# Chunked cross-attention on one core: scores and probabilities times values placed together, and every engine's list reordered

## The chip, the cores and the metric

The kernel runs on one core of a Trainium2 chip. The metric is device time in microseconds of one execution; three runs of the kernel before gave 1942.81, 1947.82 and 1955.28 us, median 1947.82 us. The profile is one further execution, whose span from first to last instruction is 1939.0 us.

## The reference

Batches of 32, channels 256, tokens 2048. Queries, keys and values all come from the context tensor; attention is within chunks of 64 tokens, with 8 heads of 32 channels.

```python
qh, kh, vh = proj(ctx, Wq, bq), proj(ctx, Wk, bk), proj(ctx, Wv, bv)   # in chunks of 64
scores = einsum('bnqhd,bnkhd->bnhqk', qh, kh) / sqrt(32)
scores = scores + where(mask > 0, 0, -1e9)
attn   = softmax(scores)
out    = einsum('bnhqk,bnkhd->bnqhd', attn, vh) @ W_out.T + b_out
out    = out.transpose(0, 2, 1) * mask + x
mu, var = mean and variance over the 2048 tokens
return (out - mu) * rsqrt(var + 1e-5)
```

## The kernel before, in words

The work is cut into 128 blocks of 512 tokens, four to a batch. Each engine runs its own straight list of instructions, written out by a Python loop `periods(step)`; one step is called a round here. In round p the engines work on different blocks at once: the projections on block p+2, the softmax on p+1, the turned probabilities on p, the product with values on p-1, the output projection on p-2. Nothing but semaphores joins the engines, and each engine goes through its list in the written order. So the order of the calls in the five `step` functions, together with the waits, is the whole schedule.

The stages of one block, in the order in which they depend on each other:

- ScalarE (ACT) rounds the context to `ctx_hi` (`split_ctx`, L458); GpSimd (POOL) forms the rest `ctx_lo` (`low_ctx`, L565). Products are made of three terms, hi by hi, hi by lo, lo by hi.
- TensorE (PE) projects keys and queries (L313, 24 matmuls) and values (L347, 24) into two banks `proj_bank`, of which each half f is emptied by ACT (`keys` L500, `queries` L491, `values` L508).
- POOL turns the mask into rows of 0 or a large negative number (`masked_keys`, L587), and ACT lays these into the four banks `score_bank` in two halves (`lay_negatives`, L470). TensorE adds the scores on top (`scores`, L386, 64 small matmuls).
- VectorE (DVE) takes the row maximum and subtracts it (`less_maximum`, L646, L650); ACT takes the exponential in two halves (`exponentials`, L478); DVE sums each half and forms reciprocals (`sum_up` L657, `reciprocals` L665); POOL multiplies in two halves (`divide`, L557).
- DVE transposes the probabilities in 32x32 squares (`turn`, L673), and eight transfers from the queue of SyncE (SP) put the squares in place (`move_probs`, L256). TensorE multiplies by the values (`probs_times_v`, L419), half of which were carried to the other partitions by two transfers (`move_values`, L241).
- ACT and DVE split the result (`high_attention` L485, `low_attention` L680), TensorE projects it (`project_out`, L370), DVE adds bias and mask (`output`, L691), POOL adds x (`add_residual`, L575), DVE gathers statistics (L700), and after four blocks ACT and POOL normalise (L520, L598) and SP stores.

Two waits matter for what follows. `lay_negatives(n, 0)` waits for `neg_done`, that is for `masked_keys(n)`, and for `less_done` of the block before. `divide(n, 0)` waits for `recip_done` of block n, which needs both halves of the exponentials of block n.

Of the kernel before, what the change touches and what calls it, by code (L numbers as in the profile page):

```python
# [14 lines left out]
HALVES = C // P  # L15
# [35 lines left out]
def attention_kernel(nc, x, ctx_in, mask, w_in_t, b_in, w_out_t, b_out, out):  # L51
    stack = ExitStack()
    with stack:
# [127 lines left out]
        def periods(step):  # L181
            for p in range(-3, ALL + 4):
                step(p)

        @block.sync
        def _(sp):
# [58 lines left out]
            def move_probs(n):  # L245
# [26 lines left out]
            def step(p):  # L272

                move_values(p + 1)
                if p >= -2:
                    load_ctx(p + 6)
                if there(p + 2):
                    sp.wait_ge(q_proj, 2 * (p + 2) + 1)
                if p >= -1:
                    load_mask(p + 3)  # L280
                if there(p + 2):
                    sp.wait_ge(q_proj, 2 * (p + 2) + 2)
                if p >= 3:
                    load_x(p - 1)
                move_probs(p)

                if p == ALL + 2:
                    for n in range(p - 7, ALL):
                        store(n)
                elif p < ALL + 2:  # L290
                    store(p - 7)
# [7 lines left out]
        def _(pe):  # L299
# [17 lines left out]

            def project_k(n, f):
                if not there(n):
                    return  # L320
                if f == 0:
                    pe.wait_ge(ctx_hi_done, 2 * (n + 1))
                    pe.wait_ge(ctx_lo_done, 2 * (n + 1) - 1)
                    if n == 0:
                        pe.wait_ge(ctx_lo_first, 1)
                wait(pe, v_f_done, 2 * (n - 1) + f + 1 if n else 0)
# [8 lines left out]
            def project_v(n, f):  # L335
                if not there(n):
                    return
                if there(n - 4):
                    pe.wait_ge(y_done, 2 * (n - 4) + f + 1)
                else:  # L340
                    pe.wait_ge(q_f_done, 2 * n + f + 1)
# [10 lines left out]
            def project_out(m, f):  # L352
# [6 lines left out]
                if there(m + 4):  # L359
                    pe.wait_ge(q_f_done, 2 * (m + 4) + f + 1)  # L360
                elif there(m + 3):
# [12 lines left out]
            def scores(n):  # L374
# [3 lines left out]
                pe.wait_ge(k_f_done, 2 * (n + 1))  # L378

                pe.wait_ge(seeded, 2 * (n + 1))  # L380
# [22 lines left out]
            def probs_times_v(n):  # L403
# [8 lines left out]
                pe.wait_ge(moved[n % MOVES], 128 * (n // MOVES + 1))  # L412
                for c in range(CPB):
# [36 lines left out]
        def _(act):  # L450
# [72 lines left out]
            def step(p):  # L523
                keys(p + 2, 0)
                split_ctx(p + 3, 0)
                keys(p + 2, 1)
                split_ctx(p + 3, 1)
                queries(p + 2, 0)
                queries(p + 2, 1)
                exponentials(p + 1, 0)  # L530
                exponentials(p + 1, 1)
                lay_negatives(p + 2, 0)
                lay_negatives(p + 2, 1)
                high_attention(p - 1)
                values(p + 2, 0)
                if p == ALL + 2:
                    for n in range(p - 7, ALL):
                        normalise(n)
                elif p < ALL + 2:
                    normalise(p - 7)  # L540
                values(p + 2, 1)
# [4 lines left out]
        def _(pool):  # L546
# [54 lines left out]
            def step(p):  # L601
                if p < 0:
                    masked_keys(p + 2)
                low_ctx(p + 3, 0)
# [3 lines left out]
                if p < ALL + 2:  # L608
                    normalise(p - 7)
# [161 lines left out]
```

## Time and profile before

| what | value |
|---|---|
| runs | 1942.81, 1947.82, 1955.28 us |
| span of the profiled execution | 1939.0 us |
| TensorE busy | 98% |
| VectorE busy | 88% |
| GpSimd busy | 78% |
| ScalarE busy | 69% |
| chain that ended last, share of TensorE | 96% |

The page prints only the span of the profiled execution; its own time is that span and what lies around it, and the median of the runs is 8.8 us above the span. A busy share counts only instructions that compute. The chain that ended last is followed backward from the last instruction, at each step to whatever released it.

### The profile page before, as it was taken

Reading aid. Unit: us, or ns where it says so; the run is one execution under the profiler, and the core shown is the slowest. Engines: PE = TensorE matmul, PEld = TensorE weight load, DVE = VectorE, ACT = ScalarE, POOL = GpSimd, SP = SyncE. Lnnn points to the kernel's source line nnn. Section 1 sums busy time; section 2 is a strip of 40 time slices with the busy share of each in tenths; the row PEclk is TensorE's granted clock in tenths of the full one; section 3 lists DMA queues with packets and bytes.
Section 4 is the critical chain, followed back from the end, with each engine's and each line's share of the span. In section 5 each row is a group of like instructions: output and inputs, shape, how many; then the busy total and the mean of one; then the engine's idle time right before and its main releaser. Section 6 shows DMA issues by size and latency. Waiting matters only on the chain.

```text
span 1939.0 us, 90624 instructions
## 1 busy us (share of the span) xinstructions
PE 1891.7 (98%) x40488; PEld 1608.1 (83%) x40488; DVE 1703.2 (88%) x1577; ACT 1330.1 (69%) x1792; POOL 1504.6 (78%) x1059
## 2 busy tenths in 40 slices
PE   7999999999999999999999999999999999999994
PEld 6888888888888888888888888888888888888882
DVE  4898889899999978998988999888899889989986
ACT  5667667767767766776777677677667767767762
POOL 4677778878888778878777887787778778778874
PEclk9999999999999999999999999999999999999997
DMA  5667778777777767777777777777777777777766
GB/s 171 159 181 215 218 206 224 215 218 223 212 220 222 213 196 217 222 215 215 221 219 212 221 222 214 222 210 215 212 221 219 215 217 216 222 209 222 208 176 195
DMA packets 242882, 409.60 MB, mean 211 GB/s; under 512 B 28992, under 2 KB 94784, under 8 KB 242496
## 3 DMA queue, kind: packets, MB, share of 16 engines
q1 hardware_dynamic: 242496, 403.82, 74.2%
q8 instruction: 320, 5.24, 1.2%
q14 instruction: 66, 0.54, 0.1%
HBM read 168.82 MB, written 67.11 MB: 122 GB/s over the span
## 4 chain that ended last, share of the span: by engine, by line
PE 96%; DVE 1%; issue 1%; ACT 1%; DMA 0%; POOL 0%; SPq 0%; DVEq 0%
PE proj_bank L313 38%; PE proj_bank L370 19%; PE proj_bank L347 19%; PE score_bank L386 11%; PE o_bank L419 9%; DMA b_cols<-b_in 0%; ACT prob L478 0%; ACT score_bank L470 0%; DVE squares L673 0%; SPq L256 0%; POOL prob L557 0%; DVE stats L700 0%; POOL y L575 0%; DMA prob_t<-squares 0%; DVE sums L657 0%
## 5 line engine op out<-in xcount | busy, mean ns | idle before, releaser
L557 POOL TENSOR_TENSOR prob<-prob,recip 128x1024 f32<-128x1024 f32 x256 | 482.0, 1904 | 46.5 <-DVE recip L665 46.5
L575 POOL TENSOR_TENSOR y<-y,x_raw 128x512 f32<-128x512 f32 x256 | 331.5, 1295 | 181.1 <-DVE y L691 181.1
L565 POOL TENSOR_TENSOR ctx_lo<-ctx_raw,ctx_hi 128x512 fp32r<-128x512 f32 x255 | 330.2, 1295 | 171.9 <-ACT ctx_hi L458 159.7
L500 ACT ACTIVATE k_f<-proj_bank,b_cols 128x512 f32<-128x512 f32 x256 | 176.4, 689 | 365.2 <-PE proj_bank L313 365.2
L646 DVE TENSOR_REDUCE row_max<-score_bank 128x32 f32<-128x2048 f32 x128 | 293.4, 2292 | 138.7 <-PE score_bank L386 138.7
L313 PE MATMUL proj_bank<-ctx_hi,w_hi 128*128 128x512 f32 x1024 | 337.1, 410 | 3.0 <-DVE ctx_lo L630 3.0
L313 PE MATMUL proj_bank<-ctx_hi,w_lo 128*128 128x512 f32 x1024 | 322.1, 396 | 0.7 <-issue 0.7
L313 PE MATMUL proj_bank<-ctx_lo,w_hi 128*128 128x512 f32 x1024 | 322.1, 396 | 0.0
L657 DVE TENSOR_REDUCE sums<-prob 128x16 f32<-128x1024 f32 x256 | 309.3, 1209 | 5.0 <-ACT prob L478 5.0
L650 DVE TENSOR_TENSOR prob<-score_bank,row_max 128x2048 f32<-128x2048 f32 x128 | 293.3, 2292 | 4.4
L673 DVE STREAM_TRANSPOSE squares<-prob 128x2048 f32<-128x2048 f32 x128 | 294.6, 2301 | 2.6 <-POOL prob L557 2.6
L478 ACT ACTIVATE prob<-prob 128x1024 f32<-128x1024 f32 x256 | 255.2, 1047 | 5.6 <-DVE prob L650 5.6
L491 ACT ACTIVATE q_f<-proj_bank,b_cols 128x512 f32<-128x512 f32 x256 | 176.4, 689 | 115.1 <-PE proj_bank L313 115.1
L470 ACT ACTIVATE score_bank<-neg_rows 128x1024 f32<-128x1024 f32 x256 | 251.3, 1016 | 0.0
L587 POOL TENSOR_SCALAR neg_rows<-mask_all 128x512 f32<-128x512 f32 x128 | 247.0, 1929 | 2.5 <-DMA mask_all<-mask 2.5
L691 DVE SCALAR_TENSOR_TENSOR y<-proj_bank,b_final,mask_all 128x512 f32<-128x512 f32 x256 | 190.3, 744 | 49.8 <-PE proj_bank L370 49.8
L313 PEld LDWEIGHTS proj_bank<-ctx_hi,w_lo 128*128 128x128 f32 x1024 | 194.0, 189 | 46.9 <-issue 1.0
L313 PEld LDWEIGHTS proj_bank<-ctx_lo,w_hi 128*128 128x128 f32 x1024 | 193.5, 189 | 45.2
L313 PEld LDWEIGHTS proj_bank<-ctx_hi,w_hi 128*128 128x128 f32 x1024 | 183.9, 189 | 46.5 <-issue 3.7
L386 PE MATMUL score_bank<-k_f,q_f 32*64 32x64 f32 x16384 | 214.7, 233 | 3.0 <-ACT score_bank L470 2.8
L386 PEld LDWEIGHTS score_bank<-k_f,q_f 32*64 32x64 f32 x16384 | 196.7, 130 | 21.3 <-issue 3.8
L419 PEld LDWEIGHTS o_bank<-prob_t,v_f 64*32 64x32 f32 x8192 | 169.8, 105 | 51.2 <-issue 51.2
(45 smaller groups left out, 3487.1 us busy)
## 6 DMA issues: line engine op xcount, KB each, us to landing
prob_t<-squares SPq DMA_DIRECT2D x1024, 128.0 KB
ctx_raw<-ctx SPq DMA_DIRECT2D x128, 512.0 KB, 4.8
x_raw<-x SPq DMA_DIRECT2D x128, 512.0 KB, 4.8
out<-y SPq DMA_DIRECT2D x128, 512.0 KB, 4.3
mask_all<-mask SPq DMA_DIRECT2D x128, 256.0 KB, 4.2
v_x<-v_f SPq DMA_DIRECT2D x256, 128.0 KB, 3.4
y<-w_in_t SPq DMA_DIRECT2D x1, 768.0 KB, 5.6
y<-w_out_t SPq DMA_DIRECT2D x1, 256.0 KB, 6.7
```

The lines of the kernel that those rows point to most:

```text
L313: last = pe.matmul(proj_bank[:, f, :], w[:, h, col + f * P:col + (f + 1) * P], c[:, n % 2, h, :], start=(a == 0 and h == 0), stop=(a == 2 ...
L347: last = pe.matmul(proj_bank[:, f, t * C:(t + 1) * C], c[:, n % 2, h, tok:tok + P], w[:, h, 2 * C:3 * C], start=(a == 0 and h == 0), stop= ...
L370: last = pe.matmul(proj_bank[:, f, :], w[:, h, f * P:(f + 1) * P], o[:, m % 2, :, h, :], start=(a == 0 and h == 0), stop=(a == 2 and h == 1))
L386: last = pe.matmul(score_bank[f * CHUNK:(f + 1) * CHUNK, r, tokens], q_f[head, n % 2, f, tokens], k_f[head, n % 2, f, tokens], start=False ...
L419: last = pe.matmul(o_bank[r * DH:(r + 1) * DH, f, c * CHUNK:(c + 1) * CHUNK], values, prob_t[keys, :, r * CPB + c, :], start=True, stop=Tr ...
L557: pool.tensor_tensor(part, part, half(slots(recip[:, n % 2, :]), i), ALU.mult).then_inc(norm_done, 1)
L565: pool.tensor_tensor(ctx_lo[:, n % 2, :, tokens], ctx_raw[:, n % BLOCKS, :, tokens], ctx_hi[:, n % 2, :, tokens].bitcast(F32), ALU.subtrac ...
L575: pool.tensor_tensor(part, part, x_raw[:, m % 2, f, :], ALU.add).then_inc(added, 1)
L646: dve.tensor_reduce(row_max[:, :].rearrange("p (r c) -> p r c", c=CPB), scores_of, AX_X, ALU.max).then_inc(max_done, 1)
L650: dve.tensor_tensor(prob[:, n % 2, :, :, :], scores_of, slots(row_max[:, :]), ALU.subtract).then_inc(less_done, 1)
L657: dve.tensor_reduce(sums[:, i * SLOTS // 2:(i + 1) * SLOTS // 2], half(prob[:, n % 2, :, :, :], i).rearrange("p r c k -> p (r c) k"), AX_X ...
L673: dve.transpose(squares[:, :, :, :], prob[:, n % 2, :, :, :].rearrange("p r c (b j) -> p b (r c) j", j=SQ)).then_inc(turned, 1)
```

## The change

On TensorE the product with values of block p-1 comes directly behind the scores of block p+1, and all waits of the two are placed ahead of the scores. The output projection of block p-1 (before: p-2) comes at the end of the round, so that product and output projection of a block fall in the same round. The projection banks are therefore handed on in another sequence: K waits for the output of block n-4, V for the queries. `turn` is cut in two halves b, each with its own semaphore count, and `move_probs` sends four transfers behind each half. ACT, POOL, DVE and SP get new orders. The loop runs two rounds fewer.

```diff
@@ periods
-            for p in range(-3, ALL + 4):
+            for p in range(-3, ALL + 2):
@@ move_probs (SP)
-                sp.wait_ge(turned, n + 1)
                 wait(sp, pv_done, n)
-                for f in range(HALVES):
-                    for a in range(2):
-                        for b in range(2):
+                for b in range(2):
+                    sp.wait_ge(turned, 2 * n + b + 1)
+                    for f in range(HALVES):
+                        for a in range(2):
@@ step (SP)
-                move_values(p + 1)
-                if p >= -2:
-                    load_ctx(p + 6)
...
+                store(p - 7)
+                if there(p + 2):
+                    sp.wait_ge(k_proj, 2 * (p + 2) + 1)
                 if p >= -2:
                     load_ctx(p + 6)
+                move_probs(p)
+                if p >= 3:
+                    load_x(p - 1)
+                move_values(p + 2)
                 if p >= -1:
                     load_mask(p + 3)
@@ step (PE)
                 met(PIECE_WAITS)
+                context_ready(p + 2)
+                rows_ready(p + 1)
+                probs_ready(p - 1)
                 scores(p + 1)
+                probs_times_v(p - 1)
                 project_k(p + 2, 0)
                 project_k(p + 2, 1)
                 project_q(p + 2, 0)
                 project_q(p + 2, 1)
                 if p == -1:
                     output_bias()
-                project_out(p - 2, 0)
-                probs_times_v(p - 1)
-                project_out(p - 2, 1)
                 project_v(p + 2, 0)
                 project_v(p + 2, 1)
+                project_out(p - 1, 0)
+                project_out(p - 1, 1)
@@ step (ACT)
+                split_ctx(p + 3, 0)
+                split_ctx(p + 3, 1)
+                high_attention(p - 1)
                 keys(p + 2, 0)
-                split_ctx(p + 3, 0)
                 keys(p + 2, 1)
-                split_ctx(p + 3, 1)
+                lay_negatives(p + 2, 0)
                 queries(p + 2, 0)
+                exponentials(p + 1, 0)
                 queries(p + 2, 1)
-                exponentials(p + 1, 0)
                 exponentials(p + 1, 1)
-                lay_negatives(p + 2, 0)
+                values(p + 2, 0)
+                values(p + 2, 1)
                 lay_negatives(p + 2, 1)
-                high_attention(p - 1)
-                values(p + 2, 0)
...
+                    normalise(p - 6)
@@ step (POOL)
                 if p < 0:
                     masked_keys(p + 2)
+                add_residual(p - 2, 0)
+                add_residual(p - 2, 1)
                 low_ctx(p + 3, 0)
                 low_ctx(p + 3, 1)
                 if p >= 0:
                     masked_keys(p + 2)
...
-                add_residual(p - 2, 0)
-                add_residual(p - 2, 1)
                 divide(p + 1, 0)
                 divide(p + 1, 1)
@@ step (DVE)
-                turn(p)
-                statistics(p - 3)
...
+                turn(p, 0)
+                turn(p, 1)
+                low_attention(p - 1)
+                statistics(p - 2)
...
-                output(p - 2, 0)
                 sum_up(p + 1, 0)
-                output(p - 2, 1)
                 sum_up(p + 1, 1)
                 reciprocals(p + 1)
-                low_attention(p - 1)
+                output(p - 1, 0)
...
+                output(p - 1, 1)
```

The list of ACT before, one round in the middle of the program (names are output<-inputs; k_f, q_f, v_f are keys, queries, values of block p+2; `prob` is block p+1, `score_bank` p+2):

```order
L500 ACTIVATE k_f<-proj_bank,b_cols 128x512 [waits rows_done,k_proj]
L458 ACTIVATE ctx_hi<-ctx_raw 128x2x256 [waits v_proj,ctx_loaded2]
L500 ACTIVATE k_f<-proj_bank,b_cols 128x512 [waits rows_done,k_proj]
L458 ACTIVATE ctx_hi<-ctx_raw 128x2x256
L491 ACTIVATE q_f<-proj_bank,b_cols 128x512 [waits q_proj] x2
L478 ACTIVATE prob<-prob 128x1024 [waits less_done] x2
L470 ACTIVATE score_bank<-neg_rows 128x1024 [waits less_done,neg_done]
L470 ACTIVATE score_bank<-neg_rows 128x1024
```

The same list after the change (its lines are six higher: L476 is `lay_negatives`, L484 `exponentials`, L497 `queries`):

```order
L491 ACTIVATE o_hi<-o_bank 128x1024 [waits out_proj,pv_done]
L506 ACTIVATE k_f<-proj_bank,b_cols 128x512 [waits rows_done,k_proj] x2
L476 ACTIVATE score_bank<-neg_rows 128x1024 [waits less_done,neg_done]
L497 ACTIVATE q_f<-proj_bank,b_cols 128x512 [waits q_proj]
L484 ACTIVATE prob<-prob 128x1024 [waits less_done]
L497 ACTIVATE q_f<-proj_bank,b_cols 128x512 [waits q_proj]
L484 ACTIVATE prob<-prob 128x1024 [waits less_done]
L514 ACTIVATE v_f<-proj_bank 128x512 [waits pv_done,v_proj] x2
L476 ACTIVATE score_bank<-neg_rows 128x1024
```

The first half of the laying of block p+2, with its wait for `neg_done`, has moved from behind both exponentials of block p+1 to ahead of both; the second half stands behind the values.

The list of POOL before, in the same place (prob is `divide`, ctx_lo is `low_ctx`, neg_rows is `masked_keys`, the two y lines are `normalise` and `add_residual`):

```order
L557 TENSOR_TENSOR prob<-prob,recip 128x1024 [waits recip_done]
L557 TENSOR_TENSOR prob<-prob,recip 128x1024
L565 TENSOR_TENSOR ctx_lo<-ctx_raw,ctx_hi 128x2x256 [waits ctx_hi_done] x2
L587 TENSOR_SCALAR neg_rows<-mask_all 128x512 [waits seeded,mask_loaded1]
L598 TENSOR_SCALAR y<-y,rstd,shift 128x512 [waits shift_done]
L575 TENSOR_TENSOR y<-y,x_raw 128x512 [waits x_loaded1,y_done]
L575 TENSOR_TENSOR y<-y,x_raw 128x512 [waits y_done]
```

And after the change (lines six higher):

```order
L563 TENSOR_TENSOR prob<-prob,recip 128x1024 [waits recip_done]
L563 TENSOR_TENSOR prob<-prob,recip 128x1024
L581 TENSOR_TENSOR y<-y,x_raw 128x512 [waits x_loaded1,y_done]
L581 TENSOR_TENSOR y<-y,x_raw 128x512 [waits y_done]
L571 TENSOR_TENSOR ctx_lo<-ctx_raw,ctx_hi 128x2x256 [waits ctx_hi_done] x2
L593 TENSOR_SCALAR neg_rows<-mask_all 128x512 [waits seeded,mask_loaded1]
L604 TENSOR_SCALAR y<-y,rstd,shift 128x512
```

The two residual additions now stand between the divisions and `masked_keys`, whose place behind `low_ctx` is kept.

## Rows read from the trace of the kernel before

**Rows 1.** The chain that ended last, one round: start, us, what.

```profile
721.09 1.40 PE proj_bank L370 x6
722.49 1.41 PE o_bank L419 x91
723.90 1.58 PE proj_bank L370 x6
725.49 2.88 PE proj_bank L347 x24
728.36 1.57 PE score_bank L386 x91
729.93 5.77 PE proj_bank L313 x24
```

**Rows 2.** Timeline of ACT in a round: start us, us, instruction.

```profile
1014.09 0.69 ACT L491 ACTIVATE q_f<-proj_bank,b_cols 128x512 f32<-128x512 f32 x1 [0.71 <-PE proj_bank L313]
1014.68 1.99 ACT L478 ACTIVATE prob<-prob 128x1024 f32<-128x1024 f32 x2
1016.57 1.96 ACT L470 ACTIVATE score_bank<-neg_rows 128x1024 f32<-128x1024 f32 x2
```

**Rows 3.** Timeline of DVE in the same part.

```profile
1019.41 1.21 DVE L657 TENSOR_REDUCE sums<-prob 128x16 f32<-128x1024 f32 x1
1020.72 0.35 DVE L665 RECIPROCAL recip<-sums 128x32 f32<-128x32 f32 x1
...
1023.10 2.29 DVE L646 TENSOR_REDUCE row_max<-score_bank 128x32 f32<-128x2048 f32 x1 [0.71 <-PE score_bank L386]
...
1027.63 2.30 DVE L673 STREAM_TRANSPOSE squares<-prob 128x2048 f32<-128x2048 f32 x1
1029.86 1.25 DVE L700 BATCH_NORM_STATS2 stats<-y 128x6 f32<-128x512 f32 x2
```

**Rows 4.** Timeline of POOL in the same part, and two additions near the end.

```profile
1021.16 3.77 POOL L557 TENSOR_TENSOR prob<-prob,recip 128x1024 f32<-128x1024 f32 x2 [0.29 <-DVE recip L665]
1025.85 2.68 POOL L565 TENSOR_TENSOR ctx_lo<-ctx_raw,ctx_hi 128x512 fp32r<-128x512 f32 x2 [0.92 <-ACT ctx_hi L458]
1028.49 1.94 POOL L587 TENSOR_SCALAR neg_rows<-mask_all 128x512 f32<-128x512 f32 x1
...
1911.30 2.53 POOL L575 TENSOR_TENSOR y<-y,x_raw 128x512 f32<-128x512 f32 x2 [3.49 <-DVE y L691]
```

**Rows 5.** Timeline of SP: eight transfers of probabilities, twice.

```profile
1884.52 5.79 SPq L256 DMA_DIRECT2D prob_t<-squares  x8
...
1909.42 4.95 SPq L256 DMA_DIRECT2D prob_t<-squares  x8
```

**Rows 6.** TensorE in stretches: us, busy (instructions), granted clock, DMA share, GB/s.

```profile
44.50:46.30 1.80, 0.06 (x1) 1.00 0.87 200
47.00:53.00 6.00, 5.33 (x95) 0.50 0.63 156
262.00:264.00 2.00, 0.44 (x43) 1.00 0.40 135
704.00:706.00 2.00, 0.00 (x0) 0.91 0.54 196
706.00:712.00 6.00, 5.70 (x36) 0.50 0.47 108
```

**Rows 7.** Who waited for whom: us in total, times, longest.

```profile
PE o_bank L419 <- issue: 6.2, 4, 2.6
```

**Rows 8.** The chain near the end of the program.

```profile
1890.53 2.30 DVE row_max L646
...
1913.78 2.44 DMA prob_t<-squares
...
1918.03 2.87 PE proj_bank L370 x6
...
1921.67 1.13 DVE o_lo L680
```

**Rows 9.** Timeline of DVE, the first row maximum.

```profile
23.95 2.29 DVE L646 TENSOR_REDUCE row_max<-score_bank 128x32 f32<-128x2048 f32 x1 [10.69 <-PE score_bank L386]
```

More of the change, by code:

```diff
@@ L272, in step @@
             def step(p):
-                move_values(p + 1)
+                store(p - 7)
+                if there(p + 2):
+                    sp.wait_ge(k_proj, 2 * (p + 2) + 1)
                 if p >= -2:
                     load_ctx(p + 6)
-                if there(p + 2):
-                    sp.wait_ge(q_proj, 2 * (p + 2) + 1)
+                move_probs(p)
+                if p >= 3:
+                    load_x(p - 1)
+                move_values(p + 2)
                 if p >= -1:
                     load_mask(p + 3)
[L281 to L288, printed above, removed]
+                if p == ALL + 1:
+                    for n in range(p - 6, ALL):
                         store(n)
-                elif p < ALL + 2:
-                    store(p - 7)
             periods(step)
@@ L315, in project_qk, with context_ready @@
                 last.then_inc(proj, 1)
+            def context_ready(n):
+                if not there(n):
+                    return
+                pe.wait_ge(ctx_hi_done, 2 * (n + 1))
+                pe.wait_ge(ctx_lo_done, 2 * (n + 1) - 1)
+                if n == 0:
+                    pe.wait_ge(ctx_lo_first, 1)
             def project_k(n, f):
@@ L320, in project_k @@
                     return
[L321 to L326, printed above, removed]
+                if there(n - 4):
+                    pe.wait_ge(y_done, 2 * (n - 4) + f + 1)
+                else:
+                    wait(pe, v_f_done, 2 * (n - 1) + f + 1 if n else 0)
                 project_qk(n, f, k_proj, C)
@@ L337, in project_v @@
                     return
[L338 to L341, printed above, removed]
+                pe.wait_ge(q_f_done, 2 * n + f + 1)
                 for t in range(2):
@@ L358, in project_out @@
                     pe.wait_ge(o_hi_done, m + 1)
-                if there(m + 4):
-                    pe.wait_ge(q_f_done, 2 * (m + 4) + f + 1)
-                elif there(m + 3):
+                if there(m + 3):
                     pe.wait_ge(v_f_done, 2 * (m + 3) + f + 1)
@@ L372, in project_out, with rows_ready @@
                 last.then_inc(out_proj, 1)
-            def scores(n):
+            def rows_ready(n):
                 if not there(n):
@@ L380, in scores @@
                 pe.wait_ge(seeded, 2 * (n + 1))
+            def scores(n):
+                if not there(n):
+                    return
                 for c in range(CPB):
@@ L412, in probs_times_v @@
                 pe.wait_ge(moved[n % MOVES], 128 * (n // MOVES + 1))
+            def probs_times_v(n):
+                if not there(n):
+                    return
                 for c in range(CPB):
@@ L607, in step @@
                     masked_keys(p + 2)
-                if p < ALL + 2:
-                    normalise(p - 7)
-                if there(p - 3) and (p - 3) % BLOCKS == BLOCKS - 1:
-                    reciprocal_std((p - 3) // BLOCKS)
-                if p == ALL + 2:
-                    for n in range(p - 7, ALL):
+                if p < ALL + 1:
+                    normalise(p - 6)
+                if there(p - 2) and (p - 2) % BLOCKS == BLOCKS - 1:
+                    reciprocal_std((p - 2) // BLOCKS)
+                if p == ALL + 1:
+                    for n in range(p - 6, ALL):
                         normalise(n)
-                add_residual(p - 2, 0)
-                add_residual(p - 2, 1)
                 divide(p + 1, 0)
@@ L665, in reciprocals, with turn @@
                 dve.reciprocal(recip[:, n % 2, :], sums[:, :]).then_inc(recip_done, 1)
-            def turn(n):
+            def turn(n, b):
                 if not there(n):
                     return
-                dve.wait_ge(norm_done, 2 * (n + 1))
-                if there(n - 1):
-                    dve.wait_ge(moved[(n - 1) % MOVES], 128 * ((n - 1) // MOVES + 1))
-                dve.transpose(squares[:, :, :, :], prob[:, n % 2, :, :, :].rearrange(
-                    "p r c (b j) -> p b (r c) j", j=SQ)).then_inc(turned, 1)
+                if b == 0:
+                    dve.wait_ge(norm_done, 2 * (n + 1))
+                    if there(n - 1):
+                        dve.wait_ge(moved[(n - 1) % MOVES], 128 * ((n - 1) // MOVES + 1))
+                dve.transpose(squares[:, b, :, :], prob[:, n % 2, :, :, b * SQ:(b + 1) * SQ].rearrange(
+                    "p r c j -> p (r c) j")).then_inc(turned, 1)
             def low_attention(m):
```

18 lines of the change are left out of this document (8 added, 10 removed).

## The prediction

> **What bounds the kernel now.** I read the page's table of busy times first, then the chain of waits, then the timelines of one round. TensorE is busy for 98% of the span, and the chain that ended last lies on it for 96%. One round of that chain [rows 1] shows six TensorE pieces end to end: 1.40 + 1.41 + 1.58 + 2.88 + 1.57 + 5.77 = 14.61 us, each beginning where the last one ended. So in the steady part TensorE never waits, 128 blocks need some 128 x 14.65 = 1875 us, and start and end make up the rest of 1939.0. The other engines idle in each round, but no chain through them is as long as TensorE's round. The question for a reordering is therefore not what it does to any one busy time (nearly nothing), but whether some loop of waits from one round to the next becomes longer than 14.65 us. A loop here is a set of instructions each waiting for the one before, which comes back to the same instruction one block on; its summed length is a floor under the time of a round, however idle the engines are.
>
> **The change on TensorE.** Before, a round goes from wide to small matmuls and back twice (values' product between the two output projections; scores between V and K). The output projection behind the product takes 1.58 us, the one that is not behind it 1.40 [rows 1]: 0.18 us for one such passage. With the product right behind the scores there is one passage fewer, so TensorE's own work becomes 14.61 - 0.18 = 14.43 us. [...] Were TensorE still the bound, a round would gain 0.18 us by the row, 23 us over 128 blocks. But the bound moves.
>
> **The loop that the change closes.** In the order listings, ACT now lays the first half of the negatives of block n ahead of both exponentials of block n-1, and waits there for `masked_keys(n)`. POOL forms `masked_keys(n)` behind the two divisions of block n-2, the two residual additions and two `low_ctx`. Those divisions need both exponentials of block n-2, which on ACT stand behind the laying of block n-1, which waited for `masked_keys(n-1)`. So from one `masked_keys` to the next, one block on, everything is in series:
>
> - ACT: laying 1.96/2 = 0.98; queries 0.59 (start of the queries to start of the exponentials); first exponential (1016.57 - 1014.68)/2 = 0.945; queries 0.59; second exponential to its end 1.99 - 0.945 = 1.045. Sum 4.15 us [rows 2].
> - DVE: second sum 1.21, 0.10 to the reciprocal, reciprocal 0.35. Sum 1.66 [rows 3].
> - POOL: divisions 3.77, additions 2.53, `low_ctx` 2.64 (start to start), `masked_keys` 1.94. Sum 10.88 [rows 4].
> - three passages from engine to engine, of 0.09 to 0.10 us each: the reciprocal ends at 1021.07 and the division starts at 1021.16 [rows 3, 4]. Sum 0.29.
>
> Together 16.98 us per block against 14.65. In the kernel before, the exponentials stood ahead of the laying, so the same path took two rounds to come back and had 29 us for it; that is why it never showed. POOL's `normalise` (and every fourth round the tiny power) stands behind `masked_keys`, beside ACT's 4.15 us, and costs nothing.
>
> **Does the rest fit into 16.98?** Count from the end M of `masked_keys(p+2)`. V half 0 needs the first queries, done at M + 0.1 + 0.98 + 0.69 = 1.8; V then ends near 4.8, the output projections near 7.6, scores 9.2, product 10.6, K and Q 16.5. The next V may start at 16.98 + 1.8 = 18.8, so TensorE stands still for about 2.2 us ahead of V in every round, and its 0.18 us are worth nothing. DVE: scores end 9.2, row maximum from 9.35, maximum and subtraction 4.53 (start to start) to 13.9, two half turns 2.2, `low_attention` 1.1, statistics 1.2, first sum 1.1, so it could start the second sum at 19.6, and the exponential lets it start at 16.98 + 4.35 = 21.3: 1.7 us to spare [rows 3]. SP: the first half turned near 15.1, eight issues of 4.95 to 5.79 us in all [rows 5], landing 2.44 us after the start of the last [rows 8]. Cutting `turn` in two lets them start some 1.1 us earlier. They have landed by 22 to 23, and the next scores wait for them at 24.6. So the second new loop (scores, maximum, turn, transfers, next scores) is 22 or 23 minus 7.6 = 14.5 to 15.5 us: also about as long as the old round, but covered by the first.
>
> **The granted clock.** Away from the end the trace has three stalls of TensorE between 1.5 and 3 us. [...] The new stall of 2.2 us lies between, and I take a fall after two in three of such stalls. Six and a half microseconds at half clock cost TensorE about 3.0 us (bounds 0 and 3.3), which first uses up the 1.7 us that DVE has to spare and every fourth round a little less to spare; 1.5 us remain per fall. A round after a fall starts V without a stall, hence no fall there: one fall in 1.5 + 1 = 2.5 rounds, 49 falls, 49 x 1.5 = 74 us.
>
> **Start and end.** The first row maximum comes at 23.95 [rows 9]; the layings now follow the values of block 0, two of 0.98 later: 25.8. The loop is not complete before there are residuals; the first three intervals come out, by the same durations, at 12.6 (in this first one the K and Q of block 1, its V, and a laying that waits for the first subtraction are in series), 15.9 and 14.3: 68.6. Then 123 intervals of 16.98 (2088.5), and one without `low_ctx`, 14.4: the last row maximum at 2171.5. From there to the end the trace took 1939.0 - 1890.5 = 48.5 us [rows 8]. An output projection of 2.87 us and the output behind it stood between `o_hi` and `o_lo` of the last block and are gone now: 46.0. Span 2217.5. The median of the runs lies 8.8 us above the span of the profile (1947.8 against 1939.0), so 2226 without clock falls and **2300 us** with them, against 1947.8: 18% slower.
>
> **Rivals.**
>
> - *The loop alone, the clock stays up* (chance 0.27). [...] Time 2226, with 0.1 us error of a handoff giving 13 us: 2200 to 2250.
> - *The forecast: loop and clock falls in part of the rounds* (0.48). The number of falls may be from 20 to 64 and their cost from 1 to 2 us: 2246 to 2350.
> - *Falls in every second round and transfers landing late besides* (0.17). If the eight transfers land 3.4 us or more after their last issue while scores are late, both loops add up: 17.9 to 18.3 us a round, 2340 to 2400.
> - *The first loop is not there* (0.03), since POOL or ACT gets ahead in a way that I do not see; then the transfer loop decides: 14.5 to 15.5 us per round, which over 124 rounds, with the same start, end and 8.8, gives 1920 to 2045 us, slower where it exceeds 14.8.
> - *TensorE remains the bound* (0.05) at 14.43 us, the end two and a half us shorter and two small stalls absent: 1948 - 23 - 3 = 1922, and 1.3% faster. It would need both loops to be at most 14.43, and against that stand POOL's 10.88 us and ACT's 4.15, which are plain sums of durations from rows.
>
> The last two share the side of faster: with all of the fifth and a part of the fourth I put 0.05 on faster by over 1%, 0.02 within 1% (which is about what measurement can tell), 0.93 on slower. The range takes the second rival whole, the forecast, and half of the third: 2200 to 2370.
>
> **What would show it.** In the profile after: TensorE busy near 14.5 of each 17 or so us, with one idle of about 2 us ahead of the V projection, ended by queries; ACT's `score_bank` (first half) waiting 2 us or more per round for POOL `neg_rows`; POOL the engine of the chain with the largest share, with 11.8 us of work and its only idle ahead of `prob` for the reciprocal; row maxima 17 to 17.7 us apart; stretches of 6 to 7 us with the granted clock at 0.50 in two rounds of five. If ACT shows no wait for `neg_rows`, the loop is wrong and so is the number; if the clock is at 1.00 throughout, the first rival holds.

## The result: 2718 us, 39% slower, and the profile after

Four runs of the changed kernel gave 2703.15 to 2737.81 us, median 2717.64; four of the kernel before 1942.81 to 1961.15, median 1951.55. The ratio is 1.394, 95% interval 1.388 to 1.400. The profiled execution took 2711.79 us, its span is 2710.0 us. The forecast was 2300 us, range 2200 to 2370: the direction held, the size did not.

The page of the changed kernel, busy time and share of the span, then the granted clock in tenths in 40 slices, then the chain's shares:

```profile
PE 2151.0 (79%) x40488; PEld 1793.5 (66%) x40488; DVE 1764.2 (65%) x1705; ACT 1304.5 (48%) x1792; POOL 1473.9 (54%) x1059
...
PEclk8888888888888898888888888888888888888887
...
PE 73%; issue 19%; DMA 3%; SPq 3%; DVE 1%; POOL 0%; ACT 0%; DVEq 0%; POOLq 0%; ACTq 0%
```

TensorE has the same 40488 matmul records, but is busy 79% and not 98%. POOL and ACT, which the forecast's loop runs through, stand at 0% of the chain. The share of "issue" was 1% before and is 19% now: time in which the engine waited for nothing that the profile shows. The table of who waited for whom has it, with total in us, number of times and longest:

```profile
POOL prob L563 <- DVE recip L671: 1116.2, 128, 13.8
...
PE o_bank L422 <- issue: 441.7, 126, 5.1
...
PE proj_bank L308 <- issue: 70.6, 63, 2.1
...
PE score_bank L385 <- DMA prob_t<-squares: 9.8, 16, 3.0
```

No row has ACT `score_bank` waiting for POOL `neg_rows`, which was the forecast's own test. One round of the chain, to be laid beside [rows 1] (L385 are the scores, L422 the product, L308 K and Q, L345 V, L366 the output projection), with the beginning of the next:

```profile
1012.04 1.58 PE score_bank L385 x84
1013.62 0.17 PE o_bank L422
1013.79 4.93 issue
1018.72 2.04 PE o_bank L422 x120
1020.76 0.72 PE proj_bank L308
1021.48 0.72 issue
1022.21 6.96 PE proj_bank L308 x23
1029.17 2.88 PE proj_bank L345 x24
1032.05 2.79 PE proj_bank L366 x12
1034.84 1.56 PE score_bank L385 x84
1036.40 0.79 PE o_bank L422 x53
1037.19 4.85 issue
```

This round is 22.8 us long; from the first scores (23.7) to the last (2662.5) the mean is 20.8. The scores are followed at once by the product, and right behind its beginning TensorE stands still for 4.93 us. After that the product takes 2.04 us instead of 1.41 and K with Q 7.7 instead of 5.77 [rows 1]: the granted clock stood at 0.50 behind the stall. In the next round the stall comes later in the product, behind 0.79 us of it. So it goes on: over the whole trace the stall begins 1.76 and 2.38 us after the scores' start, by turns, while its length varies from 1 to 5 us. The stretches, to lay beside [rows 6] (us, busy, granted clock, DMA share, GB/s):

```profile
1014.00:1019.00 5.00, 0.28 (x25) 0.62 0.35 123
1019.00:1021.00 2.00, 2.00 (x127) 0.50 0.04 8
1037.20:1042.00 4.80, 0.00 (x0) 0.70 0.29 105
```

The sum closes. The profiled spans differ by 2710.0 - 1939.0 = 771 us. TensorE's stalls without a releaser in product and K/Q grew from 6.2 + 0.7 to 441.7 + 70.6, by 505 us. Its busy time grew from 1891.7 to 2151.0, by 259 us, with the same instructions; I put that down to the lower clock (mean granted clock 0.84 against 0.99). Together 764 of 771; the remaining 7 us are the net of small waits, among them 9.8 us of the scores for the transfers.

### The profile page after: what moved, and what is told of

Same layout as the page of the kernel before. It is cut to its first block, busy times and chain, and to the rows that moved or that the text cites. A ratio compares the mean times of both kernels' runs of the same rounds, so it can differ in the third digit from the quotient of the medians.

```text
span 2710.0 us, 90622 instructions
## 1 busy us (share of the span) xinstructions
PE 2151.0 (79%) x40488; PEld 1793.5 (66%) x40488; DVE 1764.2 (65%) x1705; ACT 1304.5 (48%) x1792; POOL 1473.9 (54%) x1059
## 3 DMA queue, kind: packets, MB, share of 16 engines
q8 instruction: 320, 5.24, 0.8%
## 4 chain that ended last, share of the span: by engine, by line
PE 73%; issue 19%; DMA 3%; SPq 3%; DVE 1%; POOL 0%; ACT 0%; DVEq 0%; POOLq 0%; ACTq 0%
PE proj_bank L308 33%; PE proj_bank L345 12%; PE proj_bank L366 11%; PE o_bank L422 9%; PE score_bank L385 7%; DMA prob_t<-squares 3%; SPq L256 3%; DVE squares L680 0%; DVE row_max L652 0%; DMA b_cols<-b_in 0%; SPq L194 0%; DMA x_raw<-x 0%; POOL y L581 0%; POOL prob L563 0%; DVE prob L656 0%
## 5 line engine op out<-in xcount | busy, mean ns | idle before, releaser
L422 PE MATMUL o_bank<-prob_t,v_f 64*32 64x64 f32 x8192 | 263.0, 273 | 441.3 <-issue 439.6
L491 ACT ACTIVATE o_hi<-o_bank 128x1024 fp32r<-128x1024 f32 x128 | 131.1, 1024 | 853.6 <-PE o_bank L422 853.6
L422 PEld LDWEIGHTS o_bank<-prob_t,v_x 64*32 64x32 f32 x8192 | 201.6, 127 | 458.0 <-issue 458.0
L308 PE MATMUL proj_bank<-ctx_hi,w_hi 128*128 128x512 f32 x1024 | 444.5, 512 | 73.7 <-issue 70.6
L308 PE MATMUL proj_bank<-ctx_hi,w_lo 128*128 128x512 f32 x1024 | 396.4, 475 | 0.0
L308 PE MATMUL proj_bank<-ctx_lo,w_hi 128*128 128x512 f32 x1024 | 382.0, 460 | 0.0
L308 PEld LDWEIGHTS proj_bank<-ctx_hi,w_lo 128*128 128x128 f32 x1024 | 247.9, 242 | 150.5 <-issue 88.2
L571 POOL TENSOR_TENSOR ctx_lo<-ctx_raw,ctx_hi 128x512 fp32r<-128x512 f32 x255 | 319.3, 1273 | 11.8 <-ACT ctx_hi L464 11.8
L680 DVE STREAM_TRANSPOSE squares<-prob 128x1024 f32<-128x1024 f32 x256 | 302.2, 1218 | 2.7 <-POOL prob L563 2.7
L308 PEld LDWEIGHTS proj_bank<-ctx_hi,w_hi 128*128 128x128 f32 x1024 | 241.6, 250 | 72.5 <-issue 22.3
L308 PEld LDWEIGHTS proj_bank<-ctx_lo,w_hi 128*128 128x128 f32 x1024 | 239.0, 233 | 63.4
L484 ACT ACTIVATE prob<-prob 128x1024 f32<-128x1024 f32 x256 | 270.7, 1058 | 0.0
L476 ACT ACTIVATE score_bank<-neg_rows 128x1024 f32<-128x1024 f32 x256 | 261.6, 1022 | 0.0
L422 PE MATMUL o_bank<-prob_t,v_x 64*32 64x64 f32 x8192 | 243.7, 274 | 2.2 <-issue 2.2
```

The costliest lines, as they stand in the source:

```text
L308: last = pe.matmul(proj_bank[:, f, :], w[:, h, col + f * P:col + (f + 1) * P], c[:, n % 2, h, :], start=(a == 0 and h == 0), stop=(a == 2 ...
L422: last = pe.matmul(o_bank[r * DH:(r + 1) * DH, f, c * CHUNK:(c + 1) * CHUNK], values, prob_t[keys, :, r * CPB + c, :], start=True, stop=Tr ...
L484: act.activation(part, part, ACT.Exp, scale=SCALE).then_inc(exp_done, 1)
L571: pool.tensor_tensor(ctx_lo[:, n % 2, :, tokens], ctx_raw[:, n % BLOCKS, :, tokens], ctx_hi[:, n % 2, :, tokens].bitcast(F32), ALU.subtrac ...
L680: dve.transpose(squares[:, b, :, :], prob[:, n % 2, :, :, b * SQ:(b + 1) * SQ].rearrange("p r c j -> p (r c) j")).then_inc(turned, 1)
```

## The experiments

Two theories stood at first. **F**: TensorE outruns the fetch of its own instructions when scores and product stand together. **T/L**: a loop of waits sets the round, T through SyncE (its new wait for the first K half, then eight transfers and their landing), L through the engines' new lists. All times below are medians in us; ratios are against the kernel before on the same chip.

**e1_apart.** The product behind the K projection:

```diff
-                probs_ready(p - 1)
                 scores(p + 1)
-                probs_times_v(p - 1)
                 project_k(p + 2, 0)
                 project_k(p + 2, 1)
+                probs_ready(p - 1)
+                probs_times_v(p - 1)
@@ ACT
-                high_attention(p - 1)
                 keys(p + 2, 0)
                 keys(p + 2, 1)
+                high_attention(p - 1)
```

> The changed kernel with the product with values moved behind the K projection (48 matmul records, 2.9 us, between the two runs of small matmuls) and the o_hi copy behind the two key copies on ScalarE. Theory F (TensorE runs out of instructions: scores and product together are 512 short records in 3.1 us, and the next 16 KB of instructions come late): the stall of 2.9 to 4.9 us inside the product goes, the clock stays up, and the loop through the masked keys (16.98 us, 2226 us in all) becomes visible; 2150 to 2280 us. Theory T (SyncE's wait for the first K half, then eight transfers and 5 us of landing, close a loop of some 21 us): K ends no later, product later, so still 19 us a round or more, 2500 us or more.

Measured 2214.2 us, ratio 1.136 (1.128 to 1.145), clock 0.982. 2.9 us of wide matmuls between the two runs of small ones are worth 500 us. Three quarters of the stalls are gone (product and K together 84.0 + 55.3 us, before 512.3), and now the wait that the forecast named appears:

```profile
PE o_bank L422 <- issue: 84.0, 86, 3.5
ACT score_bank L476 <- POOL neg_rows L593: 80.5, 89, 2.8
```

**e2_before_adjacent** (the old lists, `probs_times_v(p - 1)` directly behind `scores(p + 1)`).

> The kernel before with one thing changed: the product with values stands directly behind the scores; all other engines keep their old lists. Theory F: the same stall of 3 to 5 us appears in the product in every round, the clock falls, 18 to 21 us a round, 2350 to 2700 us. Theory L (the time is set by loops through the other engines' new lists): nothing here closes a new loop, and one passage less between wide and small matmuls gives 1925 to 1950 us.

Measured 2535.9 us, ratio 1.301 (1.286 to 1.316). As a test it was confounded: the product waited 399 us for its transfers, which SyncE held behind two waits for the Q projection. It shows that this order is costly in the old lists too, but not by which of two ways: the stalls without a releaser were only 3.6 us in the product and 3.5 in K and Q. **e8_before_adjacent_free** takes those two waits of SyncE away:

```diff
-                if there(p + 2):
-                    sp.wait_ge(q_proj, 2 * (p + 2) + 1)
...
-                if there(p + 2):
-                    sp.wait_ge(q_proj, 2 * (p + 2) + 2)
```

> The kernel of e2_before_adjacent (old lists, product directly behind the scores) without SyncE's two waits for the Q projection, which in e2 held the transfers of probabilities back until they were waited for (399 us of waits of the product). Theory F (adjacent short instructions outrun the fetch of instructions): those 399 us go, but the stalls without a releaser stay at 3 us or more a round, 2300 to 2500 us. If e2's time was that SyncE loop alone: 1930 to 2000 us.

Measured 2167.9 us, ratio 1.118 (1.095 to 1.140). Adjacency, with the other engines' lists as before but for those two waits, costs 11.8%. It is less than the 2300 to 2500 us that I expected: the stalls are there 125 times in 128 rounds, but short:

```profile
PE o_bank L415 <- issue: 164.5, 125, 2.3
```

These 164.5 us and 55 us more of busy TensorE (1947.1 against 1891.7) make up 220 of the 222 us by which the span is longer. Removing the two waits without the adjacency was not run, so what it does to the data transfers' timing is not separated. In this program, then, the same adjacency costs 1.3 us of stall in a round, in the changed kernel 3.5. What else decides comes with e13.

**e3_phase** (the changed kernel, `LEAD = 166` for 102: 64 more empty waits ahead of the first round).

> The changed kernel with 64 more empty waits ahead of the first round (LEAD 166 instead of 102), so that the same instructions of a round lie a quarter of a 16 KB block later. Theory F: the length or the place of the stall changes; the time moves by over 2% either way, I guess 2550 to 2900 us. Theory T or L: 64 waits of at most 0.1 us each at the start, 2710 to 2725 us, same as the changed kernel.

Measured 2729.7 us. The time did not move by 2%, so the number expected missed; the place did. The stall is now partly inside the scores (145.5 us), and partly in the product (372.6 instead of 441.7 us). That alone did not decide. The same edit in the kernel before says more:

**e10_before_phase** (the kernel before, `LEAD = 166`, nothing else).

> The kernel before with nothing but 64 more empty waits ahead of its first round (LEAD 166 instead of 102). Theory F: a round is 640 TensorE instructions, two and a half blocks of 16 KB; the kernel before lies so that a block never falls whole into a run of short matmuls. Moved by a quarter block it does in part, and stalls of 1 to 3 us in most rounds appear: 2050 to 2350 us. Without such a mechanism: 1945 to 1960 us.

Measured 2080.8 us, ratio 1.073 (1.050 to 1.096). 64 empty waits at the very start, none inside a round, make 128 rounds 7% slower. The chain shows how, in every second round:

```profile
1028.48 1.51 PE score_bank L386 x90
1029.99 1.50 issue
1031.49 0.21 PE score_bank L386
```

No wait between engines was changed, so no loop of waits explains it. By a count of the list, what moved is where in a round an instruction block ends. The changed kernel's page shows their queue (packets, MB, share of the engines); the two pages of the kernel before, with and without the edit, have the same 320 packets and 5.24 MB:

```profile
q8 instruction: 320, 5.24, 0.8%
```

320 packets of 16 KB for 128 rounds are two and a half a round; hence every second round. The two places of the stall in the changed kernel fit this as well: they lie 0.62 us apart, and half a block is half of the product's 256 instructions, 0.7 us by its 1.41 us [rows 1] (an estimate). The size of a block comes from these traces: the packets of the queue are 16384 bytes each, and e9 below, whose page counts 74366 instructions against 90622, has 257 packets against 320, so 16256 instructions are 63 packets, 258 to one. I count with 256, from the list's 640 TensorE instructions a round and two and a half packets. The number of blocks alone does not tell the stalls: with 320 in both, those without a releaser in the product and in K and Q sum to 7 us in the kernel before and to 512 in the changed one.

**e9_half_product** (four of eight chunks left out of the product from block 1 on).

```diff
-                for c in range(CPB):
+                for c in range(CPB // 2 if n else CPB):
```

> The changed kernel with only four of the eight chunks multiplied by the values from block 1 on (the other four are left out of the product): 128 instead of 256 matmul records and 128 fewer instructions a round behind the scores, 0.74 us less matmul time. If the stall is a wait for data or another engine, the round gets 0.7 us shorter, 2620 us. Theory F: the run of short instructions takes one and a half blocks instead of two, the stall shrinks by 1.5 us or more besides and with it the clock loss: 2150 to 2500 us.

Measured 2543.7 us, ratio 1.302. The gain is 174 us, or 1.36 us a round: more than the 0.74 us of matmuls, less than theory F was to give, so the time lies outside both expectations. With 128 instructions fewer a round is two whole blocks (257 packets), so every round is alike. The stall stands in each, always 2.8 us behind the scores' start, though the product is already over. That is 0.4 us further on than in every second round of the changed kernel, where it came in the middle of the product, behind the same 1.5 us of scores and 0.79 us of product (1037.19 above):

```profile
1026.09 1.52 PE score_bank L385 x91
1027.61 0.79 PE o_bank L422 x53
1028.40 0.43 PE proj_bank L308
1028.84 4.11 issue
```

A stall that keeps its place when the product is over and a K matmul comes next is not a wait for the product's data.

**e4_no_k_wait** (SyncE's new wait removed).

```diff
-                if there(p + 2):
-                    sp.wait_ge(k_proj, 2 * (p + 2) + 1)
```

> The changed kernel without SyncE's wait for the first K half ahead of the context load and the eight transfers of probabilities. Theory T: the transfers start some 4 us earlier, the round gets shorter by 3 to 5 us, 2100 to 2350 us. Theory F: the transfers were rarely waited for (9.8 us in 16 waits), but their traffic moves to another place in the round, where it may meet the instruction blocks; 2600 to 2800 us.

Measured 2715.5 us: the same as the changed kernel. T has fallen. The transfers now start 7.5 us after the scores' start instead of some 11, and the stalls moved with them, though TensorE's list is the same: product 441.7 to 368.6 us, K and Q 70.6 to 173.8. **e7_masks_first_alone** (the changed kernel, `masked_keys(p + 2)` first in GpSimd's round):

> The changed kernel with nothing but masked_keys moved to the front of GpSimd's round: the forecast's loop is cut from 16.98 to 11.8 us. Theory F (the stall in the product and what follows it set 20.9 us a round, the loop is hidden under it): same as the changed kernel within 1.5%, 2680 to 2740 us. If the forecast's loop bound the changed kernel in any part: 2550 us or less.

Measured 2710.1 us, also the same: the forecast's loop binds nothing in the changed kernel.

**e13_store_mask_first** asks for the length of the stall. Theory G, in its expectation, is that an instruction block is fetched behind the data that were given to the transfer engines before it.

```diff
-                store(p - 7)
                 if there(p + 2):
                     sp.wait_ge(k_proj, 2 * (p + 2) + 1)
                 if p >= -2:
                     load_ctx(p + 6)
+                store(p - 7)
+                if p >= -1:
+                    load_mask(p + 3)
                 move_probs(p)
                 if p >= 3:
                     load_x(p - 1)
                 move_values(p + 2)
-                if p >= -1:
-                    load_mask(p + 3)
```

> The changed kernel with SyncE's store and mask load issued between the context load and the eight transfers of probabilities instead of behind the value transfers. Theory G (the instruction block is fetched behind the data already given to the transfer engines; in the changed kernel those are busy until 1016.4, the block then starts at 1016.45 and TensorE goes on 2.3 us later): with 0.75 MB less queued last, the stall gets 1 to 2.5 us shorter a round: 2400 to 2600 us. If data traffic plays no part: 2700 to 2740 us.

The starting point was two stretches of the changed kernel's DMA view (queue, packets, MB, share). In the first, 1013.6 to 1016.4 us, there is data alone; in the second, 1016.4 to 1018.8, almost nothing but one instruction block:

```profile
q1 hardware_dynamic: 435, 0.70, 78.4%
```

```profile
q8 instruction: 1, 0.02, 2.4%
q1 hardware_dynamic: 1, 0.00, 0.1%
```

The block starts at 1016.45 and TensorE goes on at 1018.72. In e13 the stall in the product shrank from 441.7 to 264.0 us, 1.4 us a round, as theory G said. The time did not follow, 2687.2 us: the eight transfers now start later and the scores wait for them,

```profile
PE o_bank L422 <- issue: 264.0, 126, 3.1
...
PE score_bank L385 <- DMA prob_t<-squares: 207.3, 118, 3.1
```

so its expected time missed. The transfer loop is now what bounds: the chain has SyncE's issues at 27% and the transfers at 24%.

The shortening has a rival, since TensorE now pauses ahead of the scores, about as long as the stall became shorter, and the fetch might have run on in that pause. The starts of the blocks in the traces speak against it. In the changed kernel the block behind a product stall starts 3.3 us after the scores' start (median; 0.8 to 4.8 in eight rounds of ten), in e13 1.9 us (1.1 to 2.1), in e8 1.6. In the changed kernel and e13 it never starts in a pause ahead of the scores. And TensorE goes on a nearly constant time after that start: 2.3 us in the median (2.2 to 2.7 in nine rounds of ten), in e13 2.5, in e8 2.6. In e13, for instance, a block starts at 1024.00, the stall begins at 1024.27 and ends at 1026.58. So the place in the list sets where the stall begins, and the start of a block sets when it ends. That a block starts late because data stand ahead of it is supported by e4, e13 and the two stretches, but the traces do not show when it was asked for, and which of the 16 DMA engines it shares with what, no run here shows. In e10 the blocks behind stalls start in the midst of data: the transfer engines were 0.9 busy in the 1.5 us before (median). So the waiting behind data remains the likely reason for the length, not a shown one.

**e5, e6, e11, e12, e14, e15, e16** look for the forecast's loop and for a better order. **e5_apart_masks_first** is e1 with

```diff
-                if p < 0:
-                    masked_keys(p + 2)
+                masked_keys(p + 2)
                 add_residual(p - 2, 0)
...
-                if p >= 0:
-                    masked_keys(p + 2)
```

> The kernel of e1_apart (product behind the K projection) with GpSimd's masked_keys moved from behind low_ctx to the front of its round. The forecast's loop (laying, exponentials, sum, divisions, additions, low_ctx, masked_keys; 16.98 us) is cut by the two additions and the two low_ctx, 5.2 us, to 11.8. If that loop set e1_apart's round (its mean is 16.9 us), the round falls to TensorE's 14.4 us and its remaining stalls of about 1.1 us: 1950 to 2090 us. If e1_apart was bound by anything else (the x load, SyncE), it stays within 2% of 2214 us.

Measured 2203.0 us, no change. GpSimd waited 309.5 us for the mask's load instead, so **e11_apart_masks_early** loads it a round earlier (`load_mask(p + 4)`, and `load_mask(2)` at the start).

> The kernel of e5_apart_masks_first with the mask of a block loaded one round earlier, since e5 waited 309 us for that load. If e5 and e1 are level because this wait took the place of the masked-keys loop: now 2000 to 2110 us (TensorE 14.4 us and 1 to 2 us of stalls a round). If the stalls of TensorE alone set e5's 16.9 us: within 2% of 2203 us.

Measured 2206.7 us: again level. Its chain is TensorE and "issue"; the stalls without a releaser (184.6 us) with their clock loss set 16.8 us a round there, just where the loop also stood. e1's time near 2226 was therefore no proof of the loop.

**e6_spread** puts the product back between Q and V, and lays behind the exponentials:

```diff
@@ PE
-                probs_ready(p - 1)
                 scores(p + 1)
-                probs_times_v(p - 1)
...
                 project_q(p + 2, 1)
+                probs_ready(p - 1)
+                probs_times_v(p - 1)
                 project_v(p + 2, 0)
@@ ACT
-                high_attention(p - 1)
                 keys(p + 2, 0)
                 keys(p + 2, 1)
-                lay_negatives(p + 2, 0)
                 queries(p + 2, 0)
                 exponentials(p + 1, 0)
                 queries(p + 2, 1)
                 exponentials(p + 1, 1)
+                high_attention(p - 1)
                 values(p + 2, 0)
+                lay_negatives(p + 2, 0)
@@ DVE
-                low_attention(p - 1)
                 statistics(p - 2)
...
                 sum_up(p + 1, 0)
+                low_attention(p - 1)
                 sum_up(p + 1, 1)
@@ POOL: masked_keys first, as in e5
```

> The changed kernel with masked_keys first on GpSimd, the product with values back between the Q and V projections (7.3 us behind the scores), the second half of ScalarE's list in the old order (exponentials ahead of the laying, o_hi behind them) and o_lo between the two sums on VectorE. Output projection in the same round, two rounds fewer, and the halved turn stay. Theory F and the loop theory together: nothing is left above TensorE's own 14.6 us, the end is some 3 us shorter: 1935 to 1955 us, same as the kernel before. If another loop of the new lists binds, over 1990 us.

Measured 2255.2 us: another loop bound, through the mask's load (424.3 us of waits). **e12_spread_masks_early** removes it as e11 does.

> The kernel of e6_spread with the mask loaded one round earlier (e6 waited 424 us for it, and the residual additions and statistics queued behind). If that wait set e6's round of 17.3 us: 1940 to 2030 us, near the kernel before. If not: within 2% of 2255 us.

Measured 1996.4 us, ratio 1.029 (1.009 to 1.049), as expected. **e15_spread_loop_back** puts the forecast's loop into it: `masked_keys` behind the `low_ctx`, the first laying ahead of the queries and exponentials.

> The kernel of e12_spread_masks_early with the forecast's loop put back: masked_keys again behind the two additions and two low_ctx on GpSimd, and the first laying again ahead of both exponentials on ScalarE. Forecast: 16.98 us a round, 2200 to 2250 us, with ScalarE waiting for neg_rows and GpSimd's work in the chain. If the loop does not exist as summed: within 2% of 1996 us.

Measured 2435.7 us, ratio 1.252, with the waits foreseen but well above the time expected. The wait, then one turn of the chain (the first "issue" is the time of ScalarE's laying, which ends as the queries begin):

```profile
ACT score_bank L477 <- POOL neg_rows L594: 512.5, 125, 7.3
...
1014.67 0.85 issue
1015.51 0.67 ACT q_f L498
1016.18 0.95 ACT prob L485
1017.13 0.58 ACT q_f L498
1017.71 0.94 ACT prob L485
1018.65 0.92 ACT o_hi L492
...
1019.60 1.22 DVE o_lo L688
1020.82 1.14 DVE sums L664
...
1022.05 0.36 DVE recip L672
...
1024.35 1.90 POOL prob L564
1026.25 2.49 POOL y L582 x2
1028.75 2.50 POOL ctx_lo L572 x2
1031.25 1.90 POOL neg_rows L594
```

From one end of `neg_rows` (1014.53) to the next (1033.15) it is 18.62 us. The sum said 16.98; the difference is `o_hi` and `o_lo`, 0.92 + 1.22 us, which in e12's lists stand between the exponential and the second sum (they do not in the changed kernel), less some 0.5 us by which POOL's and ACT's pieces came out shorter. So the loop exists nearly as summed; it was the expected 2200 to 2250 that forgot the two instructions.

**e14_spread_phase** (e12 with `LEAD = 86`).

> The kernel of e12_spread_masks_early with 16 fewer empty waits at the start (LEAD 86 instead of 102). In e12 a block ends two matmuls into K, 2 us after the one before it ended, and K stalls 0.4 us or more in every second round (52 us in all). Moved by 16 instructions the block ends four or five matmuls further, some 2 us later: theory F says these 52 us and some clock loss go, 1930 to 1950 us, level with the kernel before. Without the mechanism: within 0.5% of 1996 us.

Measured over six runs 1971.8 us, ratio 1.014 (1.010 to 1.018): by the medians 25 us better than e12, half or less of what I expected. e12 had two runs and an interval of 1.009 to 1.049, so the gain in time is not clear of noise; that K's stalls went from 52.3 to 5.7 us is. **e16_spread_x_first** moves `load_x(p - 1)` ahead of `move_probs(p)` in e14.

> The kernel of e14_spread_phase with the x load issued ahead of the eight transfers of probabilities. GpSimd waited 116 us for x in e14. If some of its rounds above 15.2 us (26 of 127) come from x arriving late, 1940 to 1965 us; if they are stalls of TensorE in the fetch of instructions, within 0.5% of 1972 us. Below 1940 us, and so faster than the kernel before, only if both shrink.

Measured 2006.4 us, ratio 1.034 (1.029 to 1.038), worse: stalls without a releaser in the product went from 17.8 to 49.6 us, and ACT's waits for it from 28.4 to 60.4. No order tried beats the kernel before.

## Why the prediction was wrong, point by point

That the kernel became slower was forecast, but the direction came out right by luck: the loop that the forecast rests on binds nothing in the changed kernel (e7), and what made it slower stands nowhere in the forecast.

**What bounds the kernel now.** Right: TensorE, with no idle in a round.

**The change on TensorE**, costed as one passage fewer, 0.18 us gained. This is the step that failed. I costed the adjacency by matmul durations alone and took "the bound moves" to mean another engine. In its place the runs show 3.5 us of stall in the product and 0.6 in K a round, and 2.0 us of lost clock: 6 us a round. The stalls end 2.3 us (product) and 2.4 us (K) in the median after the start of an instruction block, which is why I take them for waits for the next instructions. Part of the rows for it was in my hands. Of the three stalls that I used only to price the clock [rows 6, 7], the first, before 46.3, is a wait for ScalarE's laying:

```profile
46.30 1.04 PE L386 MATMUL score_bank<-k_f,q_f 32*64 32x64 f32 x62 [1.75 <-ACT score_bank L470]
```

But the other two, 1.64 us from 262.44 and 2.60 from 703.69, have TensorE idle in the middle of a product with no releaser. I never asked what such a wait is. They end at 264.08 and 706.30, which is 2.4 and 2.3 us after a 16 KB block started (261.64 and 704.00): the same lag as behind the changed kernel's stalls. The kernel's empty waits, `LEAD` and `PIECE_WAITS`, which wait for nothing and shift the list by whole instructions, pointed the same way.

**The loop through the masked keys**, 16.98 us. The dependences were right and the sum nearly so (e15: 18.62, of which 2.14 are instructions that only e15 has in it). But a loop is a floor, and TensorE's round of 20.8 us lay above it: e7 cuts the loop and nothing changes.

**The transfer loop**, 14.5 to 15.5 us, hidden: right (9.8 us of waits in all, e4 unchanged). But I took 2.44 us of landing from [rows 8] where the chain after has 5.15 to 5.49, and I overlooked SyncE's new wait for K, behind which the transfers start some 11 us after the scores' start and not at the turn (7.5 us, e4). With those two the loop is about as long as TensorE's stalled round. It became the bound when e13 put two issues, about one microsecond, ahead of the transfers and shortened the stall.

**The granted clock.** I forecast a fall in two rounds of five, behind a stall of 2.2 us, 74 us in all. The clock did fall behind the stalls, and in nearly every round: 1 us after their ends it stood at 0.50 behind 110 of the 126 in the product, which are 3.7 us long (median, up to 5.1). TensorE's busy time grew by 259 us. That term was more than three times too small, and the stalls behind it are not the ones forecast. The fall after two in three stalls was my estimate from the three of the kernel before [rows 6], behind which the clock stood at 0.50 (1.75 us), 1.00 (1.64) and 0.50 (2.60); no run shows it as a rate, and most of the 126 are longer stalls than that of the forecast.

**Start and end.** 46.0 us from the last row maximum (2664.1) to the end (2710.0): measured 45.9.

**The rivals.** None named the fetch of instructions. The third, clock falls and late transfers, stopped at 2400.

## What to carry to other kernels

Before placing two runs of short matmuls side by side, count their instructions against their time (here 512 in some 3 us), and look in the profile for TensorE waits with no releaser in the middle of a run. Here four of them, 6.2 us in all, were the only sign that the list already met late instruction blocks. In a list of straight code like this one, the position of a round in its instruction blocks is a parameter of its own (7% in e10), which a reordering can change, and it should be tried (a few empty instructions at the start) before an order is judged. A loop of waits summed gave a floor that held (e15: 18.62 us, against 16.98 and the 2.14 of the two instructions); it says nothing about what else lies above it.

## What the runs showed of the hardware that I had not expected

- TensorE stood still for 4.1 us (median of 125) at the same place in every round, behind the short instructions of scores and half a product, with a K matmul next (e9).
- TensorE's stalls in the product ended 2.3 us (median of 126) after a 16 KB instruction block had started; in the changed kernel such a block started at 1016.45, when the data transfers had just run dry.
- 64 empty waits ahead of the first round cost the kernel before 7.3% (1940 to 2081 us), although each round's work and waits are unchanged.
- The same adjacency costs 1.3 us of stall a round in e8 and 3.5 in the changed kernel; with the store and the mask load issued ahead of the transfers, 2.1 (e13).
- Issuing one 512 KB load ahead of eight small transfers, in an otherwise equal list, cost 1.8% (e14 against e16, intervals apart). Why was not settled.
